# Score units of the first two head groups placed earlier in two expert batches, and the first value projection placed at the end of the fourth

## The reference

```
x = x + 0.5 * ffn(layernorm(x))      # 8 experts, the best 2 of each token, and one shared expert
x = x + attn(layernorm(x))           # 16 heads of 8 features, alibi slopes, causal
x = x + 0.5 * ffn(layernorm(x))

attn: q, k, v = x @ Wq.T, x @ Wk.T, x @ Wv.T
      scores = q @ k.T / sqrt(8) - slope * rel;  masked;  softmax;  @ v;  @ Wo.T
ffn:  h = silu(x @ w1[e]);  y = h @ w2[e];  sum over e of coef[e] * y   (+ silu(gate) * up @ down, gated)
```

## Time and profile before

| | |
|---|---|
| median of 3 runs | 318.75 us (316.54 to 320.65) |
| the profiled execution | 317.94 us |
| its span, first to last instruction | 316.2 us |
| PE, DVE, ACT, POOL busy | 286.5, 251.3, 175.6, 127.7 us |
| mean granted TensorE clock | 0.968 |

### The profile page before, as it was taken

One profiled execution on the slowest core, in us unless ns is written; L12 is line 12 of the kernel. 1 busy time (PEld: TensorE's weight loads), 2 busy tenths in 40 slices (PEclk: granted clock), 3 DMA queues, 4 the chain that ended last, 5 costly groups with the idle time before them and its releaser, 6 DMA issues.

```text
span 316.2 us, 7140 instructions
## 1 busy us (share of the span) xinstructions
PE 286.5 (91%) x2328; PEld 185.6 (59%) x2328; DVE 251.3 (79%) x1039; ACT 175.6 (56%) x342; POOL 127.7 (40%) x251
## 2 busy tenths in 40 slices
PE   0889998999998898999799999999999999999994
PEld 0688886977664343334433344333443799989994
DVE  3799898889787787998778989998621698988875
ACT  2423433433555777878578888886888333334330
POOL 1355256306128623575324534666533352420200
PEclk9999999999997599999889999997999999999999
DMA  6910000660022113411113411110000001000011
GB/s 169 244 24 2 0 0 4 224 167 11 3 101 100 42 51 116 151 54 53 51 40 127 140 54 52 54 55 1 4 2 2 0 3 33 2 18 20 1 32 35
DMA packets 20668, 17.73 MB, mean 56 GB/s; under 512 B 2460, under 2 KB 19420, under 8 KB 20572
## 3 DMA queue, kind: packets, MB, share of 16 engines
q1 hardware_dynamic: 19912, 17.05, 18.0%
q10 hardware_dynamic: 720, 0.23, 0.4%
HBM read 9.74 MB, written 7.34 MB: 54 GB/s over the span
## 4 chain that ended last, share of the span: by engine, by line
PE 61%; DVE 14%; POOL 9%; issue 8%; ACT 4%; DMA 2%; SPq 1%; DVEq 0%; POOLq 0%
PE bank L904 16%; PE bank L1033 10%; PE bank L1001 8%; PE bank L839 6%; PE bank L841 5%; PE bank L840 5%; DVE X L699 4%; POOL probs L402 3%; DVE masked_s L767 2%; PE bank L974 2%; DMA X<-in_x 2%; DVE stats L622 2%; PE bank L1043 2%; ACT probs L528 2%; PE bank L1056 2%
## 5 line engine op out<-in xcount | busy, mean ns | idle before, releaser
L767 DVE CUSTOM_DVE_ANT_0 masked_s<-bank,causal_sb 128x512 f32<-128x512 f32 (+3 forms) x256 | 110.0, 486 | 16.0 <-PE bank L974 15.8
L528 ACT ACTIVATE probs<-bank 128x512 f32<-128x512 f32 x160 | 89.7, 602 | 26.0 <-PE bank L1001 25.1
L699 DVE SCALAR_TENSOR_TENSOR X<-bank,coef,X 128x128 f32<-128x128 f32 x272 | 76.2, 342 | 16.2 <-PE bank L904 13.2
L904 PEld LDWEIGHTS bank<-w_sb,act 128*128 128x128 f32 x512 | 67.3, 192 | 6.6 <-ACT act L451 1.1
L904 PE MATMUL bank<-w_sb,act 128*128 128x128 f32 x512 | 67.7, 275 | 0.6 <-ACT act L451 0.6
L402 POOL TENSOR_SCALAR_AFFINE_SELECT probs<-probs 128x512 f32<-128x512 f32 x64 | 39.8, 635 | 65.5 <-ACT probs L528 65.5
L974 PE MATMUL bank<-KA,QA 54*128 54x512 bf16 (+3 forms) x256 | 59.0, 318 | 4.8 <-DVE smax L767 4.1
L451 ACT ACTIVATE act<-bank 128x512 f32<-128x512 f32 x72 | 41.7, 594 | 37.3 <-PE bank L841 36.7
L1001 PE MATMUL bank<-QA,KA 57*128 57x128 bf16 (+3 forms) x256 | 59.3, 317 | 0.9 <-issue 0.7
L1033 PE MATMUL bank<-probs,VA 128*32 128x256 f32 (+2 forms) x640 | 53.6, 403 | 1.4 <-issue 0.9
L839 PE MATMUL bank<-XH,w_hi 128*128 128x512 f32 x88 | 42.3, 481 | 3.0 <-DVE gated L684 1.8
(11 more groups left out here) (87 smaller groups left out, 334.4 us busy)
## 6 DMA issues: line engine op xcount, KB each, us to landing
qk_scratch<-qk_parts SPq DMA_DIRECT2D x8, 384.0 KB, 2.6
QA<-qk_scratch SPq DMA_DIRECT2D x32, 96.0 KB, 2.2
KA<-qk_scratch SPq DMA_DIRECT2D x32, 96.0 KB, 2.3
qk_scratch<-qk_parts SPq DMA_DIRECT2D x8, 256.0 KB, 2.9
qk_scratch<-qk_parts SPq DMA_DIRECT2D x8, 128.0 KB, 2.8
QA<-smaxT SPq DMA_DIRECT2D x64, 3.0 KB
out_x<-X SPq DMA_DIRECT2D x4, 256.0 KB, 2.3
X<-in_x SPq DMA_DIRECT2D x3, 256.0 KB, 6.1
```

The costliest lines, as they stand in the source:

```text
L528: nc.scalar.activation(dst, src, ACT.Exp).then_inc(exp_done, 1)
L699: m = nc.vector.scalar_tensor_tensor(X[:, b * NT + t, :], Y_BANK[i % 3][:, t * P:(t + 1) * P], coef[:, j % 2, t, n:n + 1], X[:, b * NT + t ...
L767: r = nc.vector.tensor_tensor_reduce(masked_s[:, u % 4, off:off + n], bank[:, off:off + n], causal_sb[:, S - n:S], 1.0, -3e38, ALU.add, AL ...
L904: m = nc.tensor.matmul(Y_BANK[i % 3][:, r], a, w2_sb[:, n, :], start=True, stop=True)
```

## The change

The table of early score units is changed, and the value projection of batch 0 is moved:

```diff
-        EARLY_STEPS = {(2, 7): 1, (2, 8): 2, (3, 0): 2, (3, 1): 2, (3, 2): 1, (3, 3): 2, (3, 4): 2, (3, 5): 2,
-                       (3, 6): 2, (3, 7): 2, (3, 8): 2}
+        EARLY_STEPS = {(2, 7): 2, (2, 8): 2, (3, 0): 2, (3, 1): 3, (3, 2): 1, (3, 3): 3, (3, 4): 2, (3, 5): 2,
+                       (3, 6): 2, (3, 7): 1}
...
-        VALUE_SLOTS = ((0, 2), (1, 9))
+        VALUE_SLOTS = {(1, 9): 1}
...
             ffn(0)
+            values(0)
             load_table(1, ACT.Exp)
...
                     if (n, i) in VALUE_SLOTS:
-                        values(VALUE_SLOTS.index((n, i)))
+                        values(VALUE_SLOTS[n, i])
...
             ffn(0)
+            values(0)
             pe.wait_ge(up_used, B)
```

## The result

The changed kernel takes 322.09 us (median of 18 runs, 319.23 to 323.9); the kernel before, run beside it, 318.64 us (18 runs, 315.52 to 322.05). The ratio is 1.0147, 95% interval 1.0115 to 1.018: slower by 3.7 to 5.7 us. The forecast was 321.8 us, 3.1 us slower. The ratio leaves out the four slowest of the 18 runs of the kernel before, which lie more than 1.5% above its fastest; the medians of all runs differ by 3.45 us.

What follows compares the result with a forecast made beforehand. The prediction took the seam to hang on rest_qk(1, 1), which releases POOL's full chain. Lateness 0.6, 1.6, 4.0, then back to 3.1 us, clock zero: 317.94 + 3.1 = 321.0, with 0.8 for the median 321.8 us; range 316.5 to 325.5.

Steps and rivals of the forecast that it cites:

- What bounds the seam: Fourth batch's end: rest_qk(1, 1) releases POOL's back-to-back chain; from it to group 1 are 14.8 us, unaltered by the change.
- three units fewer behind the last expert and the projection placed there: Slots (3, 7) and (3, 8): costed at nothing, since the transpose can't start before POOL is done at 107.1.
- Slots (2, 7) to (3, 0), 0.6: One unit more there: its maximum on busy VectorE is paid in full, making PE 0.6 us late.
- slot (3, 1), to 1.6: Three units for two: unit 8 waits for unit 6's maxima, so the hidden layer behind is 1.6 us late.
- slot (3, 3), to 4.0: Three units for two: unit 12 waits for unit 10's maxima behind rest_qk(1, 0); hidden layer 4.0 us late.
- Slots (3, 4) to (3, 6), back to 3.1: Slot (3, 4) gives back 1.0 us, unit 16's wait adds 0.1: rest_qk(1, 1) 3.1 late, at 97.4.
- The clock: PE's clock at the seam: at best 1.1 us gained by staying full; zero taken.
- rival A: Slot (3, 3)'s stall also halves the clock: 1.7 us if short, say 5 if long; 323.5 to 327 us; chance 0.22.
- The forecast's own sign of being wrong: In the changed kernel's trace: the granted clock shows a half stretch before 95 us.
- At the seam, zero: PE's clock around the transpose and group 1: taken as zero, with a gap before the transpose either way.
- B: Batch's end is the bound, POOL's chain having slack: up to 3.8 us faster, 315 us; chance 0.10.
- C: PE's existing waits absorb both stalls, POOL starts at 95.7 as now: 318.8 us, or 317.7; chance 0.15.

Runs made afterwards that it cites:

- e7: The changed kernel with POOL's split_smax(1) put ahead of the layer norm and the last side sum; ratio 1.0039 against the kernel before.
- e2: The kernel before with only the new table of early units, the value projection left behind pair (0, 2); ratio 1.0128.
- e1: The changed kernel with the old table of early units, so only the projection is moved; ratio 0.9976 against the kernel before.
- e5: The changed kernel with VectorE's maxima of units 10 to 12 ahead of rest_qk(1, 0) in slot (3, 3); ratio 1.0073 against the kernel before.
- e10: The changed kernel with 24 matmuls of unused results filling TensorE's gap before the second transpose of the maxima; ratio 1.0214 against the kernel before.
- e3: The kernel before with three units instead of two in slot (3, 3) and one instead of two in slot (3, 8); ratio 1.0063.
- e8: Old table, projection at the fourth batch's end, POOL's split first, ACT's table load ahead of the copy to VA; ratio 0.9983 against the kernel before.
- e9: The kernel of e8 with POOL's last side sum and batch 3's addition to X behind step 0's masks and split; ratio 0.9965 against the kernel before.

## Why the prediction was right

**What bounds the seam.** Right, by two tests: the distance of 9.7 us holds whatever the table, and breaks as soon as POOL's order is changed (e7). The three units fewer behind the last expert and the projection placed there moved T1 by nothing, as costed: from `rest_qk(1, 1)` to T1 it is 9.69 us with the new table alone (e2) and 9.70 with the projection alone (e1). TensorE's wait for POOL, forecast at 3.6 us, was 4.05.

**Slots (2, 7) to (3, 0), 0.6; slot (3, 1), to 1.6; slot (3, 3), to 4.0.** Measured, in the changed kernel: 0.58 at the first unit of slot (3, 1) (77.66 against 76.64), then 1.56 and 3.97 behind the second and third. The wait of 2 us has the cause named, since turning VectorE's order round takes 1.24 us of it away (e5). The point of method: VectorE's wait of 1.76 in rows 6 was idle time nobody missed, until PE's next unit was put behind it.

**Slots (3, 4) to (3, 6), back to 3.1.** Right where the clock holds (3.07 in e2), too low by 1.4 in the execution profiled for the change, where it does not.

**The clock.** Here lay the uncertainty, and the forecast and rival A share the truth. I took "no fall" at 0.50 and "a fall" at 0.22. The forecast's own sign of being wrong, a half stretch before 95 us, did show in the profiled execution (88.3 to 91.7). The same instructions met both: full clock after the stall in e2 and e7, half in the changed kernel and e10, and half in e3 in its own form. In none of the seven profiles without that stall did the clock fall between slot (3, 3) and 96 us; so the stall goes with the fall, in three profiles of five, and does not decide it alone. The price was 1.37 between e2 and the changed kernel, near A's 1.7 for a short stretch; A's long stretch did not occur. How common the falls are was not measured: two of four profiles is too few, and the time does not tell, since the medians give 3.45 us and the ratio 4.7. The Trainium skill's rule on waits between groups of matmuls (TensorE: Matmul & The Clock Gate, "A second HAM failure mode: psum-queue depth-cycling"), which there recur in every iteration, is borne out in part: the single wait of 2 us went with the half clock in three profiles of five, the waits of 0.32 and 0.30 us of the kernel before with none.

**At the seam, zero.** The half clock came later (105) and ended later, and T3 lost another 0.70 behind T1, with 5.1 us of group 1 at the half clock instead of 2.9. I had taken zero between a gain of 1.1 and no stated loss: the term was bounded from one side only.

**The number.** 321.8 against 322.09 owes something to luck. For the profiled execution the forecast was 321.0 and the time 320.80, yet its seam was later than forecast (4.44 us at `rest_qk(1, 1)` and 5.16 at T3, for 3.1); the rest of the span happened to be 2.7 us shorter, by the half stretches of the last section. The walk's 3.1 was exceeded by the ratio (3.7 to 5.7), while the medians of all runs differ by 3.45.

**Rivals B and C** are out: neither the seam's slack (B) nor waits that would swallow the stall (C) exist. B's pricing is instructive, though: e8 and e9 took POOL's chain out of the way, with T1 3.96 and 2.29 us early, and kept about 1 us at T3.

## What to carry to other kernels

Before moving work forward into "idle" time of an engine, ask whom that engine is waiting for there, and what stands behind the moved piece on the *other* engine: a two-bank ring turned VectorE's harmless wait into a 2 us stall of TensorE. Find the one instruction that the next stage's start hangs on, and measure the distance between the two: if it is the same in every variant (9.7 us here), only that instruction's time counts for the start of that stage. And a gain of 4 us at a seam must be followed two steps further before it is believed.

## What the runs showed that I had not expected

Behind T3 all these kernels run the same program, yet the rest of the span takes from 192.2 to 198.1 us. It goes with the number of short half-clock stretches: 192.2 with none, 194.1 with one, 195.0 to 195.5 with two, 196.7 and 196.8 with three, 198.1 with four, some 1.4 us for each. (Some profiles have one more at the very end of the span, where TensorE has nothing left to do; it is not counted.) In the kernel before, the two are at 157 and 217 to 222 (stretches, columns as in rows 4):

```profile
155.00:160.00 5.00, 4.85 (x37) 2.31 (x36) 3.06 (x8) 3.15 (x6) 0.00 (x0) 0.66 0.00 0
216.00:222.00 6.00, 5.34 (x47) 1.71 (x45) 4.57 (x20) 3.73 (x8) 4.63 (x9) 0.72 0.00 1
```

and in the changed kernel there is none at these places:

```profile
155.00:160.00 5.00, 3.59 (x38) 1.49 (x36) 4.63 (x25) 3.24 (x6) 2.37 (x6) 1.00 0.25 70
216.00:224.00 8.00, 7.33 (x78) 2.51 (x78) 7.93 (x41) 6.15 (x12) 3.70 (x10) 1.00 0.01 4
```

That the time is lost in these stretches is seen in VectorE's instructions, one pair behind each place, the kernel before first:

```profile
163.14 0.69 DVE L742 SCALAR_TENSOR_TENSOR qk_rest<-bank,qk_parts 128x512 f32<-128x512 f32 x1 [0.31 <-ACT qk_parts L500]
167.45 0.69 DVE L743 SCALAR_TENSOR_TENSOR qk_rest<-bank,qk_parts 128x512 f32<-128x512 f32 x1 [0.30 <-ACT qk_parts L500]
...
222.13 0.29 DVE L767 CUSTOM_DVE_ANT_0 masked_s<-bank,causal_sb 128x128 f32<-128x128 f32 x1
224.97 0.28 DVE L768 CUSTOM_DVE_ANT_0 masked_s<-bank,causal_sb 128x128 f32<-128x128 f32 x1
```

Counted from T3 (121.25 and 126.85), the changed kernel's instruction comes 1.29 us sooner in the first pair and 2.76 in the second, 1.47 more. Up to the first place the distances from T3 are the same to 0.02, and behind the second the difference stays at 2.74 to 2.79.

This is why the one profiled span grew by only 2.9 us while its seam was 4.9 late. A spread of several us among runs of one kernel (315.5 to 322.1) could come from it too, though only the profiled executions show their stretches. A comparison of two single spans here says nothing below several us, unless the stretches are counted. What decides whether one comes is open: it was not tried.
